# A prefetch hint for the closing branch of the loops of an LSTM kernel

## The chip, the cores and the metric

The kernel runs on one core of a Trainium2 chip. The metric is the device time of one execution in microseconds (us). Before the change the median of three runs is 7890.69 us (7889.62 to 7891.22).

## What is computed

Four layers, each added to its input x of shape (4, 1024, 512), in float32:

```python
x = x + _L0_cond_ref(x, cond_1024)            # keep entries above a chosen threshold
x = x + _L1_cond_ref(x, cond_1024, Wx, Wh, b) # LSTM over 1024 time steps
x = x + _L2_cond_ref(x, cond_1024, ...)       # gated scan over time
x = x + _L3_cond_ref(x, cond_1024, Wx, Wh, b) # LSTM over 1024 time steps

# the LSTM
xW = jnp.einsum('ntd,dg->ntg', x, Wx) + b
def step(carry, xw_t):
    prev_h, prev_c = carry
    A = xw_t + prev_h @ Wh
    i = sigmoid(A[:, 0:H]); f = sigmoid(A[:, H:2*H])
    o = sigmoid(A[:, 2*H:3*H]); g = tanh(A[:, 3*H:4*H])
    next_c = f * prev_c + i * g
    next_h = o * tanh(next_c)
    return ((next_h, next_c), next_h)
```

The batch is 4, the hidden size 512, and each of the 1024 steps needs the h of the step before.

## The kernel before

The program runs five stages in order: load_and_sparsify, lstm (names with p_), gated_scan, lstm (names with q_), store. x lies in SBUF with the features on 128 partitions, in four chunks.

In lstm the 1024 steps are a loop of ROUNDS = 128 rounds of U = 8 steps. Each engine has a loop of its own (L379 on POOL, L439 on PE, L493 on ACT, L626 on DVE); the loops meet through semaphores alone, whose target values are worked out from the round's number at the top of a round. A round is two halves (v = 0, 1) of V = 4 steps, each half with its own PSUM banks.

One step, in the order in which the engines pass it on. The hidden units are two halves, A (first) and B (second):

- PE waits for h of half A (semaphore h_a) and of half B (h_b), and runs 64 matmuls for Wh (L409, h_product), which add to what bias and x have put into the banks PA and PB. Then, while the rest of the step goes on elsewhere, it runs 16 matmuls of the x part of a later half round (L402, x_product), with 8 for the bias (L397) in the first step of each half. So a round has 656 matmuls, each with a weight load.
- DVE transposes the gates out of PSUM (L597, to GT), adds the two parts of each sum (L602, both_parts, from GT and GT), forms the products (L605) and the new c (L608), h in full (L615), its high part (L618) and its low part (L623, low_h, which signals h_a or h_b). All of it is written out in one order in the loop of L626.
- ACT runs tanh and sigmoid in between (L497 to L508). Its loop stands twice in the program, in the two arms of an If; one of them runs.
- POOL adds the four h of a half round to x (L389), after h_a and h_b of its last step, and then prepares the x of a later half round (parts_of_x): L355 (x times a scale, to XC), L356 (the same rounded to 16 bits, to XH), L359 (the rest, to XH). L389 is the last instruction of each half round, so at the end of v = 1 the way from L389 to the next L355 leads over the loop's closing branch.

In POOL's half round (quoted without its waits) this reads:

```python
parts_of_x(xt_ahead[:, :, bass.ds(r * UB + v * VB, VB)], v, pool.snap(r * 2 + (v + 3)))
...
nc.gpsimd.tensor_tensor(here, here, HH[:, v].rearrange("p u (c b) -> p c u b", b=B), ALU.add).then_inc(s["xadd"], 1)
```

Of the kernel before, what the change touches and what calls it, by code (L numbers as in the profile page):

```python
# [30 lines left out]
ROUNDS = T // U  # L31
# [11 lines left out]
GA = NG // 2  # L43
USUAL = (2.0 ** -6, 1.0)
H_SCALE = 2.0 ** 7
W_TOP = 2.0 ** 13
BIG = 3.0e38

# [202 lines left out]
def lstm(nc, m, tag, x_all, weights, wh, b, wh_there, also_load=()):  # L251
# [7 lines left out]
    with ExitStack() as ctx:  # L259
# [90 lines left out]
        @block.gpsimd  # L350
        def _(pool):
            def parts_of_x(x, buf, n):
                by_step = lambda a: a.rearrange("p c (u b) -> p c u b", b=B)
                hi, lo = parts(XH[:, buf])[:, :, :, 0, :], parts(XH[:, buf])[:, :, :, 1, :]
                nc.gpsimd.tensor_tensor(XC[:], x, SXB[:], ALU.mult).then_inc(s["xscaled"], 1)  # L355
                nc.gpsimd.tensor_tensor(hi, by_step(x), by_step(SXB[:]), ALU.mult).then_inc(s["xhi"], 1)  # L356
                pool.wait_ge(s["xscaled"], n)
                pool.wait_ge(s["xhi"], n)
                nc.gpsimd.tensor_tensor(lo, by_step(XC[:]), hi, ALU.subtract).then_inc(s["xh"], 1)  # L359

            nc.gpsimd.memset(BR[:], 0.0).then_inc(s["br0"], 1)
            nc.gpsimd.memset(ONES[:], 0.0).then_inc(s["ones"], 1)
            nc.gpsimd.memset(HH[:], 0.0).then_inc(s["xadd"], 2)
            pool.wait_ge(s["ones"], 1)
            nc.gpsimd.memset(ONES[0:3, :].rearrange("p (u s b) -> p u s b", s=2, b=B)[:, :, 0, :], 1.0).then_inc(s["ones"], 1)
            for k in range(NC):
                pool.wait_ge(s["amaxk"], k + 1)
                nc.gpsimd.tensor_scalar(g_cols(stage, k), g_cols(stage, k), 2.0, None, ALU.mult).then_inc(s["dbl"], 1)
            for k in range(NC):
                pool.wait_ge(s["amaxk"], NC + k + 1)  # L370
                nc.gpsimd.tensor_scalar(g_cols(wx_sb, k), g_cols(wx_sb, k), 2.0, None, ALU.mult).then_inc(s["dbl"], 1)
            pool.wait_ge(s["amax"], 2)
            nc.gpsimd.partition_all_reduce(amaxall[:], amax[:], P, bass.bass_isa.ReduceOp.max).then_inc(s["amaxall"], 1)
            pool.wait_ge(s["sxb"], 2)
            for n in range(2):
                if n:
                    pool.wait_ge(s["xh"], n)
                parts_of_x(xt[:, :, n * VB:(n + 1) * VB], n, n + 1)
            with pool.Fori(0, ROUNDS) as r:  # L379
                for v in range(2):  # L380
                    done = pool.snap(r * 2 + (v + 1))
                    pool.wait_ge(s["xw"], done)
                    pool.wait_ge(s["xh"], pool.snap(r * 2 + (v + 2)))
                    parts_of_x(xt_ahead[:, :, bass.ds(r * UB + v * VB, VB)], v, pool.snap(r * 2 + (v + 3)))
                    ready = pool.snap(r * U + (v * V + V + 1))
                    pool.wait_ge(s["h_a"], ready)
                    pool.wait_ge(s["h_b"], ready)
                    here = xt[:, :, bass.ds(r * UB + v * VB, VB)].rearrange("p c (u b) -> p c u b", b=B)
                    nc.gpsimd.tensor_tensor(here, here, HH[:, v].rearrange("p u (c b) -> p c u b", b=B), ALU.add).then_inc(s["xadd"], 1)  # L389

        @block.tensor
        def _(pe):
            half_cols = lambda half: slice(half.at * Q, (half.at + GA) * Q)

            def bias_product(half, buf):
                for j in range(NJ):
                    nc.tensor.matmul(half.banks[buf][Q * j:Q * (j + 1), 0:GA * Q], ONES[:], BR[:, j, half_cols(half)],  # L397
                                     start=True, stop=False, skip_group_check=True)

            def x_product(half, buf, k, part):  # L400
                for j in range(NJ):
                    last = nc.tensor.matmul(half.banks[buf][Q * j:Q * (j + 1), 0:GA * Q], XH[:, buf, k, :],  # L402
                                            wx16[:, k, part, j, half_cols(half)], start=False, stop=False, skip_group_check=True)
                return last

            def h_product(half, buf, u, k, part):
                rows = 2 * B * (u + 1)
                for j in range(NJ):
                    last = nc.tensor.matmul(half.banks[buf][Q * j:Q * j + rows, 0:GA * Q], H[:, u, k, 0:rows],  # L409
                                            w16[:, part, k, j, half_cols(half)], start=False,  # L410
                                            stop=(k == NC - 1 and part == 1), skip_group_check=True)
                return last

            x_order = [(half, k, part) for half in (first, second) for k in range(NC) for part in range(2)]
            of_first = [(k, part) for k in first.ks for part in range(2)]
            of_second = [(k, part) for k in second.ks for part in range(2)]
            in_between, rest = of_first[:BETWEEN], of_first[BETWEEN:]

            pe.wait_ge(s["biasp"], 16 * 3 * NJ)
            pe.wait_ge(s["ones"], 2)  # L420
            bias_product(first, 0)
            bias_product(second, 0)
            wh_arrived(pe)
            pe.wait_ge(s["dbl"], NC)
            pe.wait_ge(s["cond"], 1)
            for k in range(NC):
                for half in (first, second):
                    for j in range(NJ):
                        last = nc.tensor.matmul(half.banks[0][Q * j:Q * j + B, 0:GA * Q], CS[:, k, :],
                                                tile_cols(stage, k, j, half.at, half.at + GA),  # L430
                                                start=False, stop=False, skip_group_check=True)
                last.then_inc(s["cond"], 1)
            pe.wait_ge(s["hi"], 2 * NC)
            pe.wait_ge(s["lo"], 2 * NC)
            pe.wait_ge(s["xh"], 1)
            for half, k, part in x_order:
                last = x_product(half, 0, k, part)
            last.then_inc(s["xw"], 1)
            with pe.Fori(0, ROUNDS) as r:  # L439
                for v in range(2):  # L440
                    for u in range(V):
                        now = pe.snap(r * U + (v * V + u + 1))
                        pe.wait_ge(s["h_a"], now)
                        for k, part in of_first:
                            h_product(first, v, u, k, part)
                        for k, part in in_between:
                            h_product(second, v, u, k, part)
                        pe.wait_ge(s["h_b"], now)
                        for k, part in of_second:
                            last = h_product(first, v, u, k, part)  # L450
                        last.then_inc(s["gates_a"], 1)
                        for k, part in rest + of_second:
                            last = h_product(second, v, u, k, part)
                        last.then_inc(s["gates_b"], 1)
                        if u == 0:
                            pe.wait_ge(s["xh"], pe.snap(r * 2 + (v + 2)))
                            bias_product(first, 1 - v)
                            bias_product(second, 1 - v)
                        for half, k, part in x_order[4 * u:4 * u + 4]:
                            last = x_product(half, 1 - v, k, part)  # L460
                        if u == V - 1:
                            last.then_inc(s["xw"], 1)

        @block.scalar
        def _(act):
# [24 lines left out]

            def steps(scale, half_scale):
                nc.scalar.activation(one_sig[:], m.eps[:], ACT.Sigmoid)
                with act.Fori(0, ROUNDS) as r:  # L493
                    for u in range(U):
                        now = act.snap(r * U + (u + 1))
                        act.wait_ge(s["pre_a"], now)
# [15 lines left out]
            with act.If(usual != 0):  # L512
                steps(1.0 / (W_TOP * H_SCALE), 0.5 / (W_TOP * H_SCALE))
            with act.Else():
# [3 lines left out]
        def _(dve):  # L518
# [30 lines left out]
            dve.wait_ge(s["exponent"], 7)  # L549
            nc.vector.tensor_scalar(em[:], em[:], H_SCALE, 2.0 ** 40, ALU.max, ALU.min).then_inc(s["exponent"], 1)  # L550
            dve.wait_ge(s["exponent"], 8)
# [71 lines left out]
                return nc.vector.scalar_tensor_tensor(nxt[:, :, B:2 * B], by_unit(HH[:, v, u, half.cols]), H_SCALE, nxt[:, :, 0:B],  # L623
                                                      ALU.mult, ALU.subtract)

            with dve.Fori(0, ROUNDS) as r:  # L626
                for v in range(2):
                    for u in range(V):
                        now = dve.snap(r * U + (v * V + u + 1))
# [293 lines left out]
```

## Time and profile before

| | us |
|---|---|
| median of three runs | 7890.69 |
| the profiled execution, its own time | 7896.71 |
| span of the profiled execution, first to last instruction | 7894.5 |
| PE busy (matmuls) | 5371.6 (68%) |
| DVE busy | 5546.4 (70%) |
| ACT busy | 2263.5 (29%) |
| POOL busy | 843.5 (11%) |

The span covers the whole program; 3536 us of it lie between the first and the last L602 of the first LSTM (247.4 to 3783.7) and as many in the second (4328.5 to 7864.5). A busy share is an average over a step in which the engines take turns. Register, branch and semaphore instructions are not counted as busy and have no rows of their own; they show only as gaps between the rows of an engine.

### The profile page before, as it was taken

Reading aid. Unit: us, or ns where it says so; the run is one execution under the profiler, and the core shown is the slowest. Engines: PE = TensorE matmul, PEld = TensorE weight load, DVE = VectorE, ACT = ScalarE, POOL = GpSimd, SP = SyncE. Lnnn points to the kernel's source line nnn. Section 1 sums busy time; section 2 is a strip of 40 time slices with the busy share of each in tenths; the row PEclk is TensorE's granted clock in tenths of the full one; section 3 lists DMA queues with packets and bytes.
Section 4 is the critical chain, followed back from the end, with each engine's and each line's share of the span. In section 5 each row is a group of like instructions: output and inputs, shape, how many; then the busy total and the mean of one; then the engine's idle time right before and its main releaser. Section 6 shows DMA issues by size and latency. Waiting matters only on the chain. (4 is left out here: it accounts for less than half of the span.)

```text
span 7894.5 us, 402402 instructions
## 1 busy us (share of the span) xinstructions
PE 5371.6 (68%) x169280; PEld 4152.5 (53%) x169280; DVE 5546.4 (70%) x35379; ACT 2263.5 (29%) x12741; POOL 843.5 (11%) x2143
## 2 busy tenths in 40 slices
PE   1577777666777777666983776667777776667776
PEld 0455555555555555555431555555555555555555
DVE  7766777776666677776678777776666777766666
ACT  4322222222222222222354222222222222222222
POOL 5100000000000000000013000000000000000000
PEclk5899999999999999999996999999999999999999
DMA  2000000000000000000001000000000000000001
GB/s 85 17 0 0 0 0 0 0 0 0 0 0 0 0 0 0 0 0 0 0 0 43 0 0 0 0 0 0 0 0 0 0 0 0 0 0 0 0 0 43
DMA packets 32261, 37.24 MB, mean 5 GB/s; under 512 B 6112, under 2 KB 22496, under 8 KB 32224
## 3 DMA queue, kind: packets, MB, share of 16 engines
q1 hardware_dynamic: 32224, 36.76, 1.4%
q8 instruction: 21, 0.34, 0.0%
q14 instruction: 16, 0.13, 0.0%
HBM read 28.34 MB, written 8.39 MB: 5 GB/s over the span
## 5 line engine op out<-in xcount | busy, mean ns | idle before, releaser
L409 PE MATMUL q_PA<-scratch,q_H 128*8 128x256 f16 (+1 forms) x32768 | 1258.3, 274 | 1058.9 <-DVE q_H L623 1058.9
L409 PE MATMUL p_PA<-scratch,p_H 128*8 128x256 f16 (+1 forms) x32768 | 1257.5, 274 | 1059.0 <-DVE p_H L623 1059.0
L409 PEld LDWEIGHTS q_PA<-scratch,q_H 128*8 128x8 f16 (+1 forms) x32768 | 647.8, 90 | 1487.4 <-DVE q_H L623 1346.8
L409 PEld LDWEIGHTS p_PA<-scratch,p_H 128*8 128x8 f16 (+1 forms) x32768 | 647.3, 90 | 1487.4 <-DVE p_H L623 1346.8
L409 PE MATMUL q_PB<-scratch,q_H 128*8 128x256 f16 (+1 forms) x32768 | 1250.1, 273 | 0.0
L409 PE MATMUL p_PB<-scratch,p_H 128*8 128x256 f16 (+1 forms) x32768 | 1249.6, 273 | 0.0
L597 DVE STREAM_TRANSPOSE q_GT<-q_PA 128x192 f32<-128x192 f32 (+1 forms) x2048 | 526.3, 295 | 744.7 <-PE q_PA L409 744.7
L597 DVE STREAM_TRANSPOSE p_GT<-p_PA 128x192 f32<-128x192 f32 (+1 forms) x2048 | 526.3, 295 | 743.8 <-PE p_PA L409 743.8
L409 PEld LDWEIGHTS q_PB<-scratch,q_H 128*8 128x8 f16 (+1 forms) x32768 | 834.7, 92 | 59.9
L409 PEld LDWEIGHTS p_PB<-scratch,p_H 128*8 128x8 f16 (+1 forms) x32768 | 834.1, 92 | 60.2
L497 ACT ACTIVATE q_GBA<-q_PREA 128x24 f32<-128x24 f32 x1024 | 194.8, 190 | 1898.0 <-DVE q_PREA L602 1898.0
L497 ACT ACTIVATE p_GBA<-p_PREA 128x24 f32<-128x24 f32 x1024 | 195.0, 190 | 1896.6 <-DVE p_PREA L602 1896.6
L597 DVE STREAM_TRANSPOSE q_GT<-q_PB 128x192 f32<-128x192 f32 (+1 forms) x2048 | 639.5, 312 | 0.0
L597 DVE STREAM_TRANSPOSE p_GT<-p_PB 128x192 f32<-128x192 f32 (+1 forms) x2048 | 639.4, 312 | 0.0
L389 POOL TENSOR_TENSOR xb<-xb,q_HH 128x64 f32 x256 | 81.9, 320 | 3164.3 <-DVE q_H L623 3164.3
L389 POOL TENSOR_TENSOR xa<-xa,p_HH 128x64 f32 x256 | 81.7, 319 | 3163.7 <-DVE p_H L623 3163.7
L602 DVE TENSOR_TENSOR q_PREA<-q_GT 128x24 f32<-128x24 f32 (+1 forms) x2048 | 368.2, 180 | 34.9
L602 DVE TENSOR_TENSOR p_PREA<-p_GT 128x24 f32<-128x24 f32 (+1 forms) x2048 | 368.0, 180 | 34.9
L738 PE MATMUL g_z<-xa,scratch 128*128 128x512 f32 x768 | 352.2, 620 | 48.2 <-DVE scratch L790 45.6
L623 DVE SCALAR_TENSOR_TENSOR q_H<-q_HH,q_H 128x8 f16<-128x8 f32 x2048 | 342.1, 167 | 35.5
L623 DVE SCALAR_TENSOR_TENSOR p_H<-p_HH,p_H 128x8 f16<-128x8 f32 x2048 | 341.9, 167 | 35.4
L615 DVE TENSOR_TENSOR p_HH<-p_SIGOB,p_TCB 128x8 f32<-128x8 f32 x1024 | 166.2, 162 | 251.9 <-ACT p_TCB L508 251.9
(220 smaller groups left out, 9260.0 us busy)
## 6 DMA issues: line engine op xcount, KB each, us to landing
scratch<-in_x_dram SPq DMA_DIRECT2D x8, 1024.0 KB, 5.4
out_dram<-xa SPq DMA_DIRECT2D x16, 512.0 KB, 6.0
xb<-in_L_cond_Wx_dram SPq DMA_DIRECT2D x8, 384.0 KB, 6.4
xb<-in_L_cond_Wh_dram SPq DMA_DIRECT2D x8, 384.0 KB, 6.2
xa<-in_L_cond_Wx_dram SPq DMA_DIRECT2D x8, 384.0 KB, 5.9
xa<-in_L_cond_Wh_dram SPq DMA_DIRECT2D x8, 384.0 KB, 6.0
xb<-in_L_cond_Wx_dram SPq DMA_DIRECT2D x8, 128.0 KB, 6.7
xb<-in_L_cond_Wh_dram SPq DMA_DIRECT2D x8, 128.0 KB, 6.5
```

The costliest lines, as they stand in the source:

```text
L389: nc.gpsimd.tensor_tensor(here, here, HH[:, v].rearrange("p u (c b) -> p c u b", b=B), ALU.add).then_inc(s["xadd"], 1)
L409: last = nc.tensor.matmul(half.banks[buf][Q * j:Q * j + rows, 0:GA * Q], H[:, u, k, 0:rows], w16[:, part, k, j, half_cols(half)], start=False,
L497: nc.scalar.activation(first.tanhs, first.pre_gif.rearrange("p (n m) -> p n m", n=3), ACT.Tanh, scale=half_scale).then_inc(s["g_a"], 1)
L597: return nc.vector.transpose(GT[:, lo:hi, :].rearrange("p g n -> p (g n)"), half.banks[v][:, (lo - half.at) * Q:(hi - half.at) * Q])
L602: return nc.vector.tensor_tensor(by_unit(dst), GT[:, lo:hi, at:at + B], GT[:, lo:hi, at + B:at + 2 * B], ALU.add)
L615: return nc.vector.tensor_tensor(HH[:, v, u, half.cols], half.sig_o[:], half.tanh_c, ALU.mult)
L623: return nc.vector.scalar_tensor_tensor(nxt[:, :, B:2 * B], by_unit(HH[:, v, u, half.cols]), H_SCALE, nxt[:, :, 0:B], ALU.mult, ALU.subtract)
L738: last = nc.tensor.matmul(banks[w * 2 + n % 2][:], wt[:, w, k, c * P:(c + 1) * P], m.xa[:, k, blk * TBB:(blk + 1) * TBB], start=(k == 0), ...
```

## The change

The four loops of lstm are opened by another call, which emits one more instruction per engine at the top of every round: a prefetch hint that names the branch which closes the loop.

```diff
+OWN = {'pe': [mybir.EngineType.PE], 'dve': [mybir.EngineType.DVE], 'act': [mybir.EngineType.Activation], 'pool': [mybir.EngineType.Pool]}
...
-            with pool.Fori(0, ROUNDS) as r:
+            with nc.Fori(0, ROUNDS, engines=OWN['pool'], hint_back_edge=True) as r:
...
-            with pe.Fori(0, ROUNDS) as r:
+            with nc.Fori(0, ROUNDS, engines=OWN['pe'], hint_back_edge=True) as r:
...
-                with act.Fori(0, ROUNDS) as r:
+                with nc.Fori(0, ROUNDS, engines=OWN['act'], hint_back_edge=True) as r:
...
-            with dve.Fori(0, ROUNDS) as r:
+            with nc.Fori(0, ROUNDS, engines=OWN['dve'], hint_back_edge=True) as r:
```

The built programs show what this adds. On POOL, in the first LSTM, the end of a round before the change (ISA stands for a few register operations fused into one instruction, REGISTER_ALU for a single one; waits are not listed):

```order
L359 TENSOR_TENSOR p_XH<-p_XC,p_XH 128x16x4
L386 REGISTER_ALU
L389 ISA
L389 TENSOR_TENSOR xa<-xa,p_HH 128x4x16
L379 REGISTER_ALU
L379 COMPARE_AND_BRANCH
```

The end of a round is the same after the change. The entry into the loop and the top of a round on POOL before:

```order
L379 UNCONDITIONAL_BRANCH
L379 ISA
L383 REGISTER_ALU
L355 ISA
L355 TENSOR_TENSOR p_XC<-xa,p_SXB 128x64
L356 TENSOR_TENSOR p_XH<-xa,p_SXB 128x16x4
L357 REGISTER_ALU
L359 TENSOR_TENSOR p_XH<-p_XC,p_XH 128x16x4
```

And after (line numbers are higher by one, for the new line of OWN):

```order
L380 UNCONDITIONAL_BRANCH
L380 BRANCH_PREFETCH_HINT
L380 ISA
L384 REGISTER_ALU
L356 ISA
L356 TENSOR_TENSOR p_XC<-xa,p_SXB 128x64
L357 TENSOR_TENSOR p_XH<-xa,p_SXB 128x16x4
L358 REGISTER_ALU
L360 TENSOR_TENSOR p_XH<-p_XC,p_XH 128x16x4
```

BRANCH_PREFETCH_HINT is new, and is the first instruction of every round, so it stands between L389 of one round and L355 of the next (L390 and L356 after the change). The loops of PE, DVE and ACT get one such row each in the same place, in both LSTMs; all other rows keep their order.

## Rows read from the trace of the kernel before

**Rows 1.** The page, its first line.

```profile
span 7894.5 us, 402402 instructions
```

**Rows 2.** Busy time by stretch; columns PE, PEld, DVE, ACT, POOL busy, PEclk, DMA, GB/s.

```profile
300.00:3780.00 3480.00, 2437.53 (x82576) 1941.51 (x82576) 2435.34 (x17120) 922.48 (x6043) 306.82 (x1008) 1.00 0.00 0
```

**Rows 3.** The waits: who waited for whom, us in total, times, longest.

```profile
PE p_PA L409 <- DVE p_H L623: 1059.0, 1023, 1.1
...
DVE p_GT L597 <- PE p_PA L409: 743.8, 1024, 4.4
...
POOL p_XC L355 <- issue: 32.7, 128, 6.7
```

**Rows 4.** Timeline of PE; first h products of three steps (start, length, what).

```profile
2011.43 0.62 PE L409 MATMUL p_PA<-scratch,p_H 128*32 128x256 f16 x16 [1.07 <-DVE p_H L623]
...
2014.88 0.61 PE L409 MATMUL p_PA<-scratch,p_H 128*8 128x256 f16 x16 [1.07 <-DVE p_H L623]
...
2018.43 0.61 PE L409 MATMUL p_PA<-scratch,p_H 128*16 128x256 f16 x16 [0.98 <-DVE p_H L623]
```

**Rows 5.** Timeline of DVE, first step of the second half of a round.

```profile
2002.54 0.52 DVE L597 STREAM_TRANSPOSE p_GT<-p_PA 128x192 f32<-128x192 f32 x2 [0.72 <-PE p_PA L409]
2002.98 0.17 DVE L602 TENSOR_TENSOR p_PREA<-p_GT 128x24 f32<-128x24 f32 x1
...
2003.41 0.18 DVE L605 SCALAR_TENSOR_TENSOR p_PRA<-p_GBA 128x16 f32<-128x16 f32 x1
```

**Rows 6.** Timeline of DVE, last instruction of a round and first step of the next.

```profile
2015.42 0.17 DVE L623 SCALAR_TENSOR_TENSOR p_H<-p_HH,p_H 128x8 f16<-128x8 f32 x1
2016.31 0.52 DVE L597 STREAM_TRANSPOSE p_GT<-p_PA 128x192 f32<-128x192 f32 x2 [0.72 <-PE p_PA L409]
2016.74 0.27 DVE L602 TENSOR_TENSOR p_PREA<-p_GT 128x24 f32<-128x24 f32 x1
...
2017.27 0.20 DVE L605 SCALAR_TENSOR_TENSOR p_PRA<-p_GBA 128x16 f32<-128x16 f32 x1
```

**Rows 7.** Timeline of POOL, in the middle of a round and at a round's top.

```profile
2002.06 0.32 POOL L389 TENSOR_TENSOR xa<-xa,p_HH 128x64 f32 x1 [12.28 <-DVE p_H L623]
2002.34 0.32 POOL L355 TENSOR_TENSOR p_XC<-xa,p_SXB 128x64 f32<-128x64 f32 x1
2002.62 0.32 POOL L356 TENSOR_TENSOR p_XH<-xa,p_SXB 128x64 f16<-128x64 f32 x1
...
2015.84 0.32 POOL L389 TENSOR_TENSOR xa<-xa,p_HH 128x64 f32 x1 [12.43 <-DVE p_H L623]
2016.36 0.32 POOL L355 TENSOR_TENSOR p_XC<-xa,p_SXB 128x64 f32<-128x64 f32 x1 [0.20 <-issue]
2016.64 0.32 POOL L356 TENSOR_TENSOR p_XH<-xa,p_SXB 128x64 f16<-128x64 f32 x1
2017.11 0.32 POOL L359 TENSOR_TENSOR p_XH<-p_XC,p_XH 128x64 f16<-128x64 f32 x1
```

**Rows 8.** Timeline of DVE, first round of the second LSTM, its first step.

```profile
4328.02 0.51 DVE L597 STREAM_TRANSPOSE q_GT<-q_PA 128x192 f32<-128x192 f32 x2 [5.65 <-PE q_PA L409]
4328.46 0.17 DVE L602 TENSOR_TENSOR q_PREA<-q_GT 128x24 f32<-128x24 f32 x1
...
4331.47 0.51 DVE L597 STREAM_TRANSPOSE q_GT<-q_PA 128x192 f32<-128x192 f32 x2 [0.72 <-PE q_PA L409]
```

**Rows 9.** Timeline of POOL, first round of the second LSTM.

```profile
4326.30 0.32 POOL L355 TENSOR_TENSOR q_XC<-xb,q_SXB 128x64 f32<-128x64 f32 x1 [13.83 <-PE q_PB L402]
...
4327.05 0.32 POOL L359 TENSOR_TENSOR q_XH<-q_XC,q_XH 128x64 f16<-128x64 f32 x1
```

**Rows 10.** Timeline ahead of the second LSTM's loop, DVE and POOL.

```profile
4299.46 10.67 DVE L583 SCALAR_TENSOR_TENSOR scratch<-xa,q_sch,scratch 128x512 f16<-128x512 f32 x16
...
4300.73 9.58 POOL L355 TENSOR_TENSOR q_XC<-xb,q_SXB 128x64 f32<-128x64 f32 x1 [6.79 <-issue]
```

**Rows 11.** The page, DMA queues that carry instructions: packets, MB, share.

```profile
q8 instruction: 21, 0.34, 0.0%
q14 instruction: 16, 0.13, 0.0%
```

**Rows 12.** Timeline of ACT, first instruction of a round.

```profile
2017.05 0.19 ACT L497 ACTIVATE p_GBA<-p_PREA 128x24 f32<-128x24 f32 x1 [1.93 <-DVE p_PREA L602]
```

## The prediction

> **What bounds the kernel now.** The span is 7894.5 us [rows 1]. I read the busy time by stretch first: in 3480 us of the first LSTM, PE and DVE are each busy for about 70%, and ACT and POOL far less [rows 2]. No engine is full, so the order of waits decides. The table of waits gives it: PE waits for DVE's new h in 1023 of 1024 steps of one LSTM, 1059.0 us in all, and DVE waits for PE's gates in all 1024 steps, 743.8 us [rows 3]. The two take turns, and a step is one lap of that chain. What the change touches can cost time only where it sits on this lap, or slows something on it.
>
> The timeline shows what a lap lasts and where a round begins. PE starts the h products of the last step of a round at 2011.43, of the first step of the next round at 2014.88 and of its second step at 2018.43 [rows 4]. The step ahead of the back edge lasts 3.45 us, the one after it 3.55. The back edges of the four engines lie in the 3.45, and PE's idle time there is the same 1.07 us as one step earlier [rows 4]: the branch itself delays nothing. The odd 0.10 us comes after it, in the first step.
>
> DVE's rows place it. In the middle of a round the first sum of a step (L602, two operands in SBUF) takes 0.17 us [rows 5]. In the first step of a round the same instruction takes 0.27, and it ends at 2017.01 [rows 6]. POOL explains the difference. Behind the h addition of L389 it prepares the next x in three operations, L355, L356 and L359. In the middle of a round L355 starts 0.28 us after L389, and L356 ends at 2002.94, ahead of L602's start at 2002.98 [rows 5, 7]. At a round's top POOL takes its back edge between L389 and L355: the pitch is 0.52, and L356 lies from 2016.64 to 2016.96, right over L602, which ends 0.05 later [rows 6, 7]. L605 behind it takes 0.20 for 0.18, with L359 ending beside it [rows 5 to 7]. A control stands in the same trace: in the first round, which has no back edge ahead of it, POOL is through by 4327.37, L602 takes 0.17 and the step 3.45 [rows 8, 9]. That POOL and DVE hold each other up is plain in the weight preparation too, where one L355 takes 9.58 us while DVE runs 16 two-operand instructions of L583 back to back [rows 10].
>
> So the trace shows one cost of the back edges, some 0.10 us a round through POOL's lateness, and 128 rounds in each of two LSTMs.
>
> **The change, part by part.** Every engine gets one hint instruction at the top of every round: 128 x 2 on each of PE, DVE, ACT and POOL. Nothing else is added, removed or moved.
>
> What it is meant to save: a fetch of code at the back edge. The two instruction queues moved 21 and 16 packets in the whole span [rows 11]; a fetch at each back edge of one engine alone would make 256. Nothing is fetched again in a round, so there is nothing to save: 0 us. The Trainium skill, page "Runtime: NRT & Kernel Launch", section "Instruction fetch mechanics", says that a taken branch whose target is not in the fetched window waits for a fetch, and gives PE room for 2048 instructions. PE's loop (656 matmuls with a weight load each, some 1320 instructions) fits into that, so the trace and the page's size agree; the page's warning, taken alone, speaks for a gain, and is rival 2.
>
> What it costs, engine by engine. The trace of before has no hint, so its price is bounded by POOL's back edge. Between L389 and L355 POOL's sequencer handles five instructions at a round's top (loop count, branch, three of register operations) in a pitch of 0.52 us, and two (a wait, one of register operations) in the middle of a round in 0.28, which is POOL's own pace, since L355 to L356 with none between is 0.28 as well [rows 7]. Three instructions more make 0.24, or 0.08 each, the taken branch among them. A hint is a plain instruction, so I take 0.06, between 0 (all of it covered, or a branch that gets shorter by as much) and 0.10 (0.52 over five). The Trainium skill, page "Advanced Engine Details and Errata", section "Control Flow Timing", gives about 51 ns for a plain branch; by that price the sum below would be 13 us in place of 15.
>
> PE: it idles 1.07 us before a round's first product [rows 4]; covered. ACT: it idles 1.93 us [rows 12]; covered. DVE: its last instruction of a round starts at 2015.42, the next at 2016.31, after 0.72 us idle that PE's gates end [rows 6]; if its back edge takes no more than POOL's 0.52, some 0.37 us is left, and a hint of 0.10 is covered. Without that cover each would add its full length to every round, 256 x 0.06 = 15 us an engine.
>
> POOL: it has 12 us to spare in a half round, so nobody waits for its result. But its three operations start later by the hint, and they are what L602 collides with. L356 starts at 2016.64 and L602 at 2016.74, so POOL is 0.10 ahead [rows 6, 7]. With 0.06 more POOL is still ahead, L356 ends at about +0.06, L602 ends 0.05 behind it as now, and all that follows in the step, L359 against L605 too, shifts by the same 0.06. The step after the back edge goes from 3.55 to 3.61. Round 0 is free of it, since POOL waits there 13.83 us for PE [rows 9].
>
> Sum: 2 x 127 rounds x 0.06 = 15.2 us, and with 0.03 to 0.09 a round 7.6 to 22.9 us. The profiled execution lasted 7896.71 us, 2.2 more than its span [rows 1], so it would be 7911.9. It lies 6.0 us above the median of the runs, 7890.69; for that median the forecast is 7905.9, with 7898 to 7914 of its own.
>
> **The rivals.**
>
> Rival 1, faster: POOL loses the race. If the hint takes more than the 0.10 us by which L356 leads, L602 is first at the shared operands and takes its 0.17 again. L356 then waits and runs beside DVE's transpose (L597), which reads PSUM; L359 slips behind the next DVE sums. The first step falls back to 3.45: 254 x 0.10 = 25 us less, 7865. For it: the lead is as short as my upper bound, and L355's 9.58 us shows that POOL is the one that waits where DVE runs back to back [rows 10]. Against it: three instructions with a branch among them made only 0.24. It decides at a hint of 0.10. The Trainium skill, page "SBUF — State Buffer", on the shared port pair, says that whichever of a GpSimd operation and a two-input DVE operation starts first holds the pair for the whole instruction and the other one blocks; by that rule L602 gains all or loses all, and the rows of L602 and of L355 agree with it. A version of it that lands L359 on L608 would cost again what it gave; I count that with rival 4.
>
> Rival 2, faster: the hint makes the taken branch on POOL shorter by more than it costs itself, be it by a fetch after all or by a target known early. L355 would come up to 0.24 us sooner, and from 0.10 on L602 is free: again 25 us less, 7865. For it: POOL's idle time ahead of L355 is booked as "issue", 32.7 us in 128 rounds, with no releaser [rows 3]. Against it: five instructions fill that gap without any stall, and nothing was fetched again [rows 11].
>
> Rival 3, no change: the hint does nothing that shows. It is handled while POOL still runs L389, or its length is 0.03 or less: 0 to 8 us, 7891 to 7898.
>
> Rival 4, slower by more: the cover on DVE is shorter than 0.37, or the hint is longer than a plain instruction, for instance by setting off a fetch each time. Every 0.1 us beyond the cover is 256 x 0.1 = 26 us: 7916 and up.
>
> **How the numbers follow.** Forecast 0.55, rival 1 0.18, rival 2 0.06, rival 3 0.13, rival 4 0.08. A measurement of this kernel tells about 0.2% from no change, 15.8 us, or 0.062 us a round. The forecast sits at that line, so its chance is halved: 0.28 within, 0.27 above. Faster: rivals 1 and 2 less a little, 0.23. Same: 0.28 with rival 3 and that little, 0.42. Slower: 0.27 and rival 4, 0.35. The range has to hold rival 1 beside the forecast and rival 3 to reach 8 in 10, as those two alone have 0.68: from 7862 (25 us and a little less than the median) to 7916 (0.10 us a round more). Rival 4 lies beyond it.
>
> **What would show it.** Right: at a round's top POOL's L389 to L355 has a pitch of about 0.58, L602 there takes about 0.33, the step from PE's first to second products 3.61, all other steps 3.44 to 3.45; PE, ACT and DVE idle as before at the back edge; the instruction queues still have some 21 and 16 packets. Wrong by rival 1: L602 back at 0.17 and L356 stretched or late. Wrong by rival 2: a pitch below 0.42. Wrong by rival 3: pitch and L602 unchanged. Wrong by rival 4: the step before the back edge longer than 3.45, or hundreds of packets in the instruction queue. The prediction as a whole is wrong if the time moves while L602 of the first step does not.

## The result and the profile after

The changed kernel takes 7908.1 us (median of 15 runs, 7906.14 to 7910.56), the kernel before, run beside it, 7892.21 us (15 runs, 7889.62 to 7895.73). That is 15.9 us more, a ratio of 1.002 with a 95% interval of 1.0012 to 1.0028. The forecast was 15.2 us more.

The page of the changed kernel, its first line and the two instruction queues:

```profile
span 7907.4 us, 403426 instructions
...
q8 instruction: 21, 0.34, 0.0%
q14 instruction: 16, 0.13, 0.0%
```

There are 1024 instructions more than in [rows 1], four engines by 256 rounds: the hints are there. The queues carried what they carried before [rows 11], so the hints fetched nothing and saved no fetch.

The timeline of POOL at a round's top (start, length, what, idle time before it). Lines are one higher than before: L390 is the h addition, L356, L357 and L360 prepare x.

```profile
2019.48 0.32 POOL L390 TENSOR_TENSOR xa<-xa,p_HH 128x64 f32 x1 [12.41 <-DVE p_H L624]
2020.07 0.32 POOL L356 TENSOR_TENSOR p_XC<-xa,p_SXB 128x64 f32<-128x64 f32 x1 [0.27 <-issue]
2020.36 0.32 POOL L357 TENSOR_TENSOR p_XH<-xa,p_SXB 128x64 f16<-128x64 f32 x1
2020.83 0.32 POOL L360 TENSOR_TENSOR p_XH<-p_XC,p_XH 128x64 f16<-128x64 f32 x1
```

The pitch from the start of the addition to the start of the first x operation is 0.59 us, where it was 0.52 [rows 7]. The idle time in it went from 0.20 to 0.27. These are rows of one round with two decimals; in the mean over the 254 round tops of both LSTMs that have a back edge ahead of them, the pitch went from 0.524 to 0.590, so a hint on POOL takes 0.066 us. The table of waits, which adds the idle time up over the 128 rounds of the first LSTM, went from 32.7 us [rows 3] to 40.9, which is 0.064 a round:

```profile
POOL p_XC L356 <- issue: 40.9, 128, 6.7
```

The timeline of DVE beside it:

```profile
2019.07 0.17 DVE L624 SCALAR_TENSOR_TENSOR p_H<-p_HH,p_H 128x8 f16<-128x8 f32 x1
2019.95 0.51 DVE L598 STREAM_TRANSPOSE p_GT<-p_PA 128x192 f32<-128x192 f32 x2 [0.72 <-PE p_PA L410]
2020.39 0.33 DVE L603 TENSOR_TENSOR p_PREA<-p_GT 128x24 f32<-128x24 f32 x1
...
2020.98 0.20 DVE L606 SCALAR_TENSOR_TENSOR p_PRA<-p_GBA 128x16 f32<-128x16 f32 x1
```

The idle time ahead of the first transpose is 0.72 us, ended by PE, as before: DVE's hint is covered. The first sum (L603, before L602) takes 0.33 us, where it took 0.27 [rows 6] and takes 0.17 in an ordinary step [rows 5]. It ends at 2020.72, 0.04 behind the end of L357 (2020.68). POOL started L357 0.03 ahead of the sum (2020.36 and 2020.39); of the lead of 0.10 us before the change, the hint used 0.07.

PE's first h products around the round's top:

```profile
2015.08 0.62 PE L410 MATMUL p_PA<-scratch,p_H 128*32 128x256 f16 x16 [1.07 <-DVE p_H L624]
2018.52 0.61 PE L410 MATMUL p_PA<-scratch,p_H 128*8 128x256 f16 x16 [1.08 <-DVE p_H L624]
...
2022.14 0.61 PE L410 MATMUL p_PA<-scratch,p_H 128*16 128x256 f16 x16 [1.04 <-DVE p_H L624]
```

The step that holds the back edges lasts 3.44 us, the one behind it 3.62, for 3.45 and 3.55 in [rows 4]. In the mean over the same 254 rounds, from DVE's first transpose of one step to that of the next, the step behind the back edge went from 3.556 to 3.618 us. 0.062 us in each of 254 rounds are 15.7 us, to hold against the 15.9 of the medians and the interval of 9.5 to 22.1 that the ratio gives. ACT's wait for the sum grew by the same 0.06 (1.99 us for 1.93 in [rows 12]).

### The profile page after: what moved, and what is told of

It reads as the page before. It is cut to its first block and busy times, and to the rows that moved or that the text cites. A ratio compares the mean times of both kernels' runs of the same rounds, so it can differ in the third digit from the quotient of the medians.

```text
span 7907.4 us, 403426 instructions
## 1 busy us (share of the span) xinstructions
PE 5373.6 (68%) x169280; PEld 4156.0 (53%) x169280; DVE 5558.6 (70%) x35379; ACT 2269.8 (29%) x12741; POOL 845.7 (11%) x2143
## 5 line engine op out<-in xcount | busy, mean ns | idle before, releaser
L390 POOL TENSOR_TENSOR xb<-xb,q_HH 128x64 f32 x256 | 82.1, 321 | 3160.5 <-DVE q_H L624 3160.5
L390 POOL TENSOR_TENSOR xa<-xa,p_HH 128x64 f32 x256 | 82.2, 321 | 3159.8 <-DVE p_H L624 3159.8
L603 DVE TENSOR_TENSOR q_PREA<-q_GT 128x24 f32<-128x24 f32 (+1 forms) x2048 | 375.5, 183 | 34.9
L603 DVE TENSOR_TENSOR p_PREA<-p_GT 128x24 f32<-128x24 f32 (+1 forms) x2048 | 375.4, 183 | 34.8
L624 DVE SCALAR_TENSOR_TENSOR q_H<-q_HH,q_H 128x8 f16<-128x8 f32 x2048 | 341.5, 167 | 35.4
L624 DVE SCALAR_TENSOR_TENSOR p_H<-p_HH,p_H 128x8 f16<-128x8 f32 x2048 | 341.5, 167 | 35.4
L616 DVE TENSOR_TENSOR q_HH<-q_SIGOB,q_TCB 128x8 f32<-128x8 f32 x1024 | 166.4, 163 | 251.6 <-ACT q_TCB L509 251.6
```

The costliest lines, as they stand in the source:

```text
L603: return nc.vector.tensor_tensor(by_unit(dst), GT[:, lo:hi, at:at + B], GT[:, lo:hi, at + B:at + 2 * B], ALU.add)
L616: return nc.vector.tensor_tensor(HH[:, v, u, half.cols], half.sig_o[:], half.tanh_c, ALU.mult)
```

## The experiments

Theory: a hint costs its length on the sequencer of its engine, and that is covered everywhere; only on POOL it makes the x operations later, and they hold up DVE's first sum by as much. Rivals: every hint costs a little on its own engine; DVE's or PE's hint delays the step; the first step is longer for a reason of its own, such as a fetch.

### The hint on POOL alone

```diff
-            with pool.Fori(0, ROUNDS) as r:
+            with nc.Fori(0, ROUNDS, engines=OWN['pool'], hint_back_edge=True) as r:
```

> The kernel before with the hint in POOL's loop alone; PE, DVE and ACT have none. Theory (the hint makes POOL's x preparation later, and DVE's first sum of the round waits for it): all of the change's loss is here, +16 us against before (+13 to +20, ratio about 1.002); in the profile POOL's pitch from the h addition to the first x operation at a round's top is 0.59 us, DVE's first sum of the round 0.34 us, the step after the back edge 3.62 us. Rival (every hint costs a little on its own engine, four shares): +4 us, and a sum of 0.27 to 0.30 us. Rival (it is DVE's or PE's hint that delays the step): 0 us, sum 0.27, pitch 0.52.

Measured: 7912.68 us beside 7898.89 for before on the same chip, 13.8 us more, ratio 1.0018 (1.0009 to 1.0027). From the timelines of POOL and DVE at a round's top:

```profile
2020.55 0.33 POOL L390 TENSOR_TENSOR xa<-xa,p_HH 128x64 f32 x1 [12.42 <-DVE p_H L624]
2021.13 0.32 POOL L356 TENSOR_TENSOR p_XC<-xa,p_SXB 128x64 f32<-128x64 f32 x1 [0.27 <-issue]
```

```profile
2021.45 0.33 DVE L603 TENSOR_TENSOR p_PREA<-p_GT 128x24 f32<-128x24 f32 x1
```

The pitch is 0.58 and the sum 0.33, as with all four hints. POOL's hint alone makes the loss; four equal shares would have made some 4 us, and the interval of the ratio begins at 7.

### The hint on PE, DVE and ACT, none on POOL

```diff
-            with pe.Fori(0, ROUNDS) as r:
+            with nc.Fori(0, ROUNDS, engines=OWN['pe'], hint_back_edge=True) as r:
...
-                with act.Fori(0, ROUNDS) as r:
+                with nc.Fori(0, ROUNDS, engines=OWN['act'], hint_back_edge=True) as r:
...
-            with dve.Fori(0, ROUNDS) as r:
+            with nc.Fori(0, ROUNDS, engines=OWN['dve'], hint_back_edge=True) as r:
```

> The kernel before with the hint in the loops of PE, DVE and ACT; POOL has none. Theory: 0 us against before (within 4 us), POOL's pitch 0.52, DVE's first sum of a round 0.27, the step after the back edge 3.55 us, and every step that ends at the back edge 3.44 to 3.45 as before. Rival (four shares): +12 us. Rival (DVE's or PE's hint): +16 us.

Measured: 7896.72 us beside 7898.89, ratio 0.9998 (0.9989 to 1.0007): no loss that can be told, and at most some 5.5 us by the interval, where the two rivals wanted 12 and 16. The timeline of DVE, last instruction of a round and first of the next:

```profile
2015.17 0.17 DVE L624 SCALAR_TENSOR_TENSOR p_H<-p_HH,p_H 128x8 f16<-128x8 f32 x1
2016.06 0.51 DVE L598 STREAM_TRANSPOSE p_GT<-p_PA 128x192 f32<-128x192 f32 x2 [0.72 <-PE p_PA L410]
2016.50 0.27 DVE L603 TENSOR_TENSOR p_PREA<-p_GT 128x24 f32<-128x24 f32 x1
```

The 0.72 us ended by PE and the 0.27 us of the sum are those of [rows 6], and the step behind the back edge has the mean of before, 3.556 us. So no cost of these three hints shows.

### POOL's loop turned, without and with hints

If the branch costs time only through the collision, then taking it out of the way between addition and preparation must win back the 0.10 us that the kernel before loses already. Turned, a round is add, prepare, add, prepare, with one preparation ahead of the loop and one at its end that nobody uses.

```diff
+            xt_later = x_all[:, 2 * VB + UB:2 * VB + UB + NC * XCOLS].rearrange("p (c n) -> p c n", c=NC)
+            pool.wait_ge(s["xw"], 1)
+            pool.wait_ge(s["xh"], 2)
+            parts_of_x(xt_ahead[:, :, 0:VB], 0, 3)
             with pool.Fori(0, ROUNDS) as r:
                 for v in range(2):
-                    done = pool.snap(r * 2 + (v + 1))
-                    pool.wait_ge(s["xw"], done)
-                    pool.wait_ge(s["xh"], pool.snap(r * 2 + (v + 2)))
-                    parts_of_x(xt_ahead[:, :, bass.ds(r * UB + v * VB, VB)], v, pool.snap(r * 2 + (v + 3)))
                     ready = pool.snap(r * U + (v * V + V + 1))
+                    pool.wait_ge(s["xw"], pool.snap(r * 2 + (v + 2)))
+                    pool.wait_ge(s["xh"], pool.snap(r * 2 + (v + 3)))
+                    count = pool.snap(r * 2 + (v + 4))
...
+                    ahead = xt_ahead[:, :, bass.ds(r * UB + VB, VB)] if v == 0 else xt_later[:, :, bass.ds(r * UB, VB)]
+                    parts_of_x(ahead, 1 - v, count)
```

> No hints. POOL's loop is turned by half a turn: the first x preparation of the loop stands ahead of it, and a round is add, prepare, add, prepare, so that the closing branch follows the last x operation, ahead of 12 us of waiting, and no longer lies between an addition and a preparation. One preparation more is made at the end, which nobody uses. Theory (the branch on POOL costs time only by making the x operations collide with DVE's first sum): at both halves the pitch is 0.28 us, the first sum 0.17 us, all steps 3.44 to 3.45 us, and the time is 25 to 30 us below before, 7862 to 7867 (ratio about 0.9965). Rival (the first step of a round is longer for another reason, such as a fetch or DVE's and PE's own branch): no change, 7892, the step still 3.55 us.

> The turned POOL loop of the run before this one, with the hint in all four loops. Theory: the hint is covered by waiting on every engine, POOL's too, and costs nothing: the same time as the turned loop without hints, within 4 us, 25 to 30 us below before. Rival (a hint costs its own length wherever it stands): 16 us above the turned loop without hints, that is 10 to 15 us below before.

Measured beside the 7898.89 us of before: 7870.93 us without hints and 7870.99 with all four, each 0.9966 (0.9952 to 0.9979), 28.0 and 27.9 us less. The timelines of POOL, DVE and PE of the turned loop without hints, at a round's top, where the preparation stood behind the branch before (L392 is the addition there, L607 the first sum; the last row of POOL is its next addition):

```profile
2008.87 0.32 POOL L392 TENSOR_TENSOR xa<-xa,p_HH 128x64 f32 x1 [12.42 <-DVE p_H L628]
2009.15 0.32 POOL L355 TENSOR_TENSOR p_XC<-xa,p_SXB 128x64 f32<-128x64 f32 x1
2009.43 0.32 POOL L356 TENSOR_TENSOR p_XH<-xa,p_SXB 128x64 f16<-128x64 f32 x1
...
2022.64 0.32 POOL L392 TENSOR_TENSOR xa<-xa,p_HH 128x64 f32 x1 [12.41 <-DVE p_H L628]
```

```profile
2009.34 0.52 DVE L602 STREAM_TRANSPOSE p_GT<-p_PA 128x192 f32<-128x192 f32 x2 [0.72 <-PE p_PA L414]
2009.78 0.17 DVE L607 TENSOR_TENSOR p_PREA<-p_GT 128x24 f32<-128x24 f32 x1
```

```profile
2007.91 0.61 PE L414 MATMUL p_PA<-scratch,p_H 128*8 128x256 f16 x16 [1.07 <-DVE p_H L628]
...
2011.35 0.61 PE L414 MATMUL p_PA<-scratch,p_H 128*16 128x256 f16 x16 [0.86 <-DVE p_H L628]
```

The pitch is 0.28, L356 ends at 2009.75, ahead of the sum at 2009.78, the sum takes 0.17 and the step 3.44. The odd step is gone (its mean over the rounds is 3.443 us, for 3.556 before), although DVE, PE and ACT still have their back edges ahead of it: the place of POOL's branch was its cause. The second run shows the rest: behind the last x operation of a round POOL waits some 12 us (12.41 in its last row), and there its hint costs nothing that shows.

### POOL later by more than a hint

Does the sum wait because POOL comes first, or because POOL works beside it at all? Waits that are long fulfilled, put at the top of POOL's round, make POOL later without a hint (the pages count 512, 768, 1280 and 2304 instructions more than before for 2, 4, 8 and 16 waits, that is 2, 3, 5 and 9 a round, so the pitch is read from the profile).

```diff
             with pool.Fori(0, ROUNDS) as r:
                 for v in range(2):
+                    if v == 0:
+                        for _ in range(2):    # 4, 8 and 16 in the other runs
+                            pool.wait_ge(s["xadd"], 2)
```

> No hints. At the top of every POOL round, ahead of the x preparation, two waits that are long fulfilled (on xadd). They only take time on POOL's sequencer, an unknown few hundredths of a us each, and make the x operations later. Theory: whatever pitch comes out, the step after the back edge is longer than 3.55 us by exactly what the pitch has more than 0.52, as long as POOL still starts ahead of DVE's first sum (lead 0.10 us before the change); with a pitch of 0.55 to 0.58 the time is 8 to 15 us above before. Rival (the hint's own kind of work cost the 16 us, such as a prefetch, not POOL's lateness): a delay without a hint costs nothing, 0 us.

> The same with four fulfilled waits. Theory: if the pitch stays below 0.62, 15 to 25 us above before; if it is beyond 0.62 us, DVE's first sum starts first, is back at 0.17 us, and the time falls to 7870 to 7880. Rival (no race: POOL delays DVE by its work whichever starts first): the sum stays long and the loss goes on growing, 25 us and more. Rival (only the hint costs): 0 us.

> The same with eight fulfilled waits. Theory: the pitch is beyond 0.62 us, so DVE's first sum is through first with 0.17 us, POOL's second x operation waits for it, and the step after the back edge is 3.45 to 3.50 us unless the third x operation lands on a later DVE sum: 10 to 28 us below before. Rival (no race): 30 us and more above before. Rival (only the hint costs): 0 us.

> The same with sixteen fulfilled waits. Theory: POOL's operations now lie among DVE's later sums of the same step (products, c, output gate), each of which can be held up to 0.3 us: between 28 us below before and 40 us above, as they fall; which DVE instruction is long in the profile is the one that a POOL operation started just ahead of. Rival (no race): above the run with eight waits by what the pitch grew. Rival (only the hint costs): 0 us.

Measured, each beside the 7897.67 us of before; pitch, long DVE instruction and step are read in the timeline, near 2000 us in the first LSTM and 6000 in the second where the two differ:

| waits | us | ratio | pitch, us | what DVE has long at the round's top | step behind the back edge, us |
|---|---|---|---|---|---|
| 2 | 7902.01 | 1.0006 (0.9996 to 1.0015) | 0.65 | second sum 0.35 for 0.20 | 3.57 |
| 4 | 7898.56 | 1.0001 (0.9992 to 1.0011) | 0.74; 0.71 | first sum 0.20 for 0.17 (first LSTM), c (L608 before) 0.27 for 0.17 | 3.58; 3.55 |
| 8 | 7887.68 | 0.9988 (0.9978 to 0.9997) | 0.90; 1.01 | products 0.23 for 0.18; second sum 0.32 | 3.50; 3.55 |
| 16 | 7933.02 | 1.0046 (1.0029 to 1.0063) | 1.26; 1.35 | products 0.27, c 0.27, a later sum 0.28; second sum 0.32, products 0.26 | 3.75; 3.65 |

With two waits the second x operation lost the race. POOL, then DVE, of that run at a round's top (L605 stands for the sums, L611 for c):

```profile
2017.47 0.32 POOL L392 TENSOR_TENSOR xa<-xa,p_HH 128x64 f32 x1 [12.42 <-DVE p_H L626]
2018.12 0.32 POOL L355 TENSOR_TENSOR p_XC<-xa,p_SXB 128x64 f32<-128x64 f32 x1 [0.33 <-POOL xa L392]
2018.40 0.33 POOL L356 TENSOR_TENSOR p_XH<-xa,p_SXB 128x64 f16<-128x64 f32 x1
2018.87 0.32 POOL L359 TENSOR_TENSOR p_XH<-p_XC,p_XH 128x64 f16<-128x64 f32 x1
```

```profile
2018.38 0.17 DVE L605 TENSOR_TENSOR p_PREA<-p_GT 128x24 f32<-128x24 f32 x1
...
2018.90 0.35 DVE L605 TENSOR_TENSOR p_PREB<-p_GT 128x32 f32<-128x32 f32 x1
```

The first sum started at 2018.38, 0.02 ahead of L356, and takes its 0.17: it is who starts first that counts. POOL's L356, 0.02 behind, takes 0.33 for 0.32, so it is hardly held in turn. Yet the run is not faster. L359 starts 0.03 ahead of the second sum and holds that up until 2019.25, 0.06 behind its own end. My expectation of 8 to 15 us more fell, since the pitch came out longer than I had supposed; the step is 0.02 longer and the time 4.3 us more, which its interval does not tell from nothing. With four waits I expected 7870 to 7880 us and got 0.9 us more than before: there c is held up. POOL, then DVE, with four waits:

```profile
2019.63 0.33 POOL L359 TENSOR_TENSOR p_XH<-p_XC,p_XH 128x64 f16<-128x64 f32 x1
```

```profile
2019.71 0.27 DVE L611 SCALAR_TENSOR_TENSOR p_GBA<-p_PRA 128x8 f32<-128x8 f32 x1
```

The first sum is not quite free there either: L355, the first x operation, started 0.17 ahead of it (2018.87 and 2019.04), and it takes 0.20. Only with eight is a part of the 28 us to be had, and with sixteen three DVE instructions are hit in one step (POOL's L355, L356 and L359 start at 2001.37, 2001.65 and 2002.15, each less than 0.12 ahead of one of them):

```profile
2001.45 0.27 DVE L608 SCALAR_TENSOR_TENSOR p_PRA<-p_GBA 128x16 f32<-128x16 f32 x1
...
2001.76 0.27 DVE L611 SCALAR_TENSOR_TENSOR p_GBA<-p_PRA 128x8 f32<-128x8 f32 x1
...
2002.22 0.28 DVE L605 TENSOR_TENSOR p_PREA<-p_GT 128x8 f32<-128x8 f32 x1
```

The steps account for the times. With sixteen waits 127 x 0.19 + 127 x 0.09 = 36 us against steps of 3.56, and 35.4 were measured; with eight, 127 x 0.06 = 8 us less, and 10.0 less were measured. A delay without any hint costs as much as its collisions, so neither the hint's own kind of work nor DVE's or PE's branch is needed to explain the loss. What it is that the operations of the two engines share is not shown by these runs; they show that it goes by who starts first.

## Why the prediction was right

**No fetch to save**: right. The two queues carry the same packets after as before, and the turned loop runs the same with and without hints.

**The price of a hint**: taken as 0.06 us between 0 and 0.10; it is 0.066 on POOL by the mean pitch, 0.064 by the waits. That it came so close is in part luck: the working gave 0.08 for an instruction, the branch among them, and 0.10 as the bound, and the 0.06 was chosen below them with no row of its own. At 0.08 the same sum would have been 20 us, still inside the interval of the measurement. The runs with waits bear out that a hint is handled like any plain instruction: their pitch grew by 0.06 to 0.09 us for each instruction added (an estimate: growth of the pitch, mean of both LSTMs, over the 2, 3, 5 and 9 instructions).

**Covered on PE, ACT and DVE**: right within what can be told: the run with these three alone has a ratio of 0.9998 and the steps of before. On DVE the cover was only estimated, at 0.37 us; the run shows that DVE's hint fits.

**Passed on one to one through POOL**: right. In the means, pitch up by 0.066, first sum up by 0.063 (0.268 to 0.331), step up by 0.062. POOL kept 0.03 to 0.04 of its lead of 0.10.

**The sum**: 15.2 us forecast, 15.9 measured, and 254 x 0.062 = 15.7 by the steps. The difference lies far inside the interval of the measurement, so it asks for no cause.

**Rival 1** did not come to pass, as the hint stayed below the lead, but its mechanism is real: at a pitch of 0.65 the first sum is through first. Its price was wrong. I gave it the whole 25 us, and counted the third operation's landing on L608 with rival 4; the runs with two and four waits show that the third operation, on the second sum or on c, takes all of it back (7902.01 and 7898.56 us beside 7897.67). It also had L356 waiting, and L356 took 0.33 us for 0.32. **Rival 2** falls, as the pitch grew, **rival 3** falls by the pitch too, and **rival 4** by the idle times at the back edge, which are those of before.

The cost that the argument found on the way, 0.10 us a round already lost before the change, was the larger matter: moving the branch took out 28 us. That is more than 254 x 0.10 = 25, because the odd step had 0.11 us too much in the mean: it fell from 3.556 to 3.443, and 254 x 0.113 are 28.7. The held sum makes 0.10 of it; that the products, 0.20 for 0.18 while L359 runs, make the rest is likely and was not tried alone.

## What to carry to other kernels

An instruction on an engine with time to spare is not free when what stands behind it can hold up the engine that sets the pace: look at what will start later, and beside what it will then lie. Put a loop's closing branch, and anything added to it, ahead of the engine's long wait and not between two pieces of work that belong together. Before trying to make code fetches cheaper, count the packets in the instruction queues against the number of rounds.

## What was not expected

How sharp the race is. With POOL 0.03 us ahead (0.41 and 0.44 behind the first transpose) DVE's sum is held for all of POOL's operation, 0.33 us; with POOL 0.02 behind it takes 0.17. The other rounds agree: in the changed kernel POOL leads by 0.02 to 0.05 us in all 254 and the sum takes 0.33 to 0.35; with two waits POOL is behind by 0.01 to 0.04 in all 254 and the sum takes 0.17. And POOL's pitch, raised in steps from 0.52 to some 1.3 us, moves the kernel from 10 us faster to 35 slower, not in one direction.

The two LSTMs have the same source, yet with eight and sixteen waits their pitches differ (0.90 and 1.01, 1.26 and 1.35 us); what makes the difference was not tried.

In the profiled execution of the changed kernel the ordinary steps were a little shorter than in that of the kernel before (a mean of 3.439 us for 3.441, from the starts of the transposes over both LSTMs), so that its span grew by 12.9 us and not by the 15.7 that the first steps add; why is open. The run with the hint on POOL alone has ordinary steps as before (3.442), its first steps add 16.5 us, and its span, 7911.4 us, is 16.9 above that of [rows 1].
